# Which engine copies the transposed probabilities in the third attention's loop: two of four on VectorE instead of one of four

## The reference

```python
def _L3_attn_ref(hidden_states, Wq, Wkv, Wo, bo):
    ...
    scores = jnp.einsum('bqhd,bkhd->bhqk', q * scale, k).astype(jnp.bfloat16)
    probs = jax.nn.softmax(scores, axis=-1)
    out = jnp.einsum('bhqk,bkhd->bqhd', probs.astype(jnp.float32), v)
    out = out.astype(jnp.bfloat16)
    out = out.reshape(B, S, H * dh).astype(jnp.float32)
    return out @ Wo + bo
```

## Time and profile before

| what | us |
|---|---|
| median of 3 runs | 673.28 |
| lowest and highest | 672.97 and 673.38 |
| the profiled execution's own time | 673.09 |
| its span (first to last instruction) | 671.3 |
| PE, DVE, ACT, POOL busy in the span | 611.6, 537.1, 398.6, 147.8 |
| copies L1406 on ACT: 24, each | 1.019 |
| copies L1611 on DVE: 8, each | 0.687 |

### The profile page before, as it was taken

How to read it: one execution, slowest core, us unless ns; L and a number is a source line. 1 busy time by engine, 2 the same in 40 slices (tenths; PEclk the granted TensorE clock), 3 DMA queues, 4 the chain that set the end, 5 groups by cost and what they waited for, 6 DMA issues and landing times. The chain is left out here.

```text
span 671.3 us, 9998 instructions
## 1 busy us (share of the span) xinstructions
PE 611.6 (91%) x3186; PEld 483.3 (72%) x3186; DVE 537.1 (80%) x1150; ACT 398.6 (59%) x785; POOL 147.8 (22%) x114
## 2 busy tenths in 40 slices
PE   6998959988899999999998899999857899999996
PEld 4685457785678888887877777777746578888784
DVE  2637589957778877888697799999969689999986
ACT  3523221102878888888864798999953445555552
POOL 0093456656311101111012011111103011111200
PEclk9698597998999999999997555555558889999998
DMA  5000000001312220221000000000001232222210
GB/s 180 1 0 1 0 1 0 1 1 64 109 65 81 96 95 21 73 94 63 0 1 0 1 2 0 0 0 0 1 1 48 82 124 77 101 83 94 83 36 31
DMA packets 9699, 28.78 MB, mean 43 GB/s; under 512 B 960, under 2 KB 3264, under 8 KB 9536
## 3 DMA queue, kind: packets, MB, share of 16 engines
q1 hardware_dynamic: 9664, 28.34, 12.2%
HBM read 27.15 MB, written 1.18 MB: 42 GB/s over the span
## 5 line engine op out<-in xcount | busy, mean ns | idle before, releaser
L1264 DVE TENSOR_TENSOR hL<-hraw,hH 128x1024 fp32r<-128x1024 f32 (+1 forms) x128 | 131.4, 1053 | 33.4 <-ACT hH L1020 32.8
L1090 PE MATMUL ps<-xH,wH 128*128 128x512 f32 x256 | 104.3, 407 | 4.8 <-DVE hraw L1194 3.0
L1024 ACT ACTIVATE hraw<-ps,bias 128x512 f32<-128x512 f32 x128 | 86.6, 686 | 29.3 <-PE ps L1092 24.8
L1091 PE MATMUL ps<-xL,wH 128*128 128x512 f32 x256 | 103.0, 402 | 0.0
L1092 PE MATMUL ps<-xH,wL 128*128 128x512 f32 x256 | 102.8, 402 | 0.0
L955 POOL TENSOR_TENSOR wL<-wraw,wH 128x1024 fp32r<-128x1024 f32 (+1 forms) x16 | 36.4, 2272 | 235.0 <-DVE wH L1141 235.0
L1102 PE MATMUL ps<-hH,wH 128*128 128x512 f32 x192 | 76.2, 397 | 7.3 <-DVE hL L1264 7.3
L1104 PE MATMUL ps<-hH,wL 128*128 128x512 f32 x192 | 76.0, 396 | 0.0
L1103 PE MATMUL ps<-hL,wH 128*128 128x512 f32 x192 | 75.7, 394 | 0.0
L1029 ACT ACTIVATE hraw<-ps 128x512 f32<-128x512 f32 x64 | 38.3, 600 | 52.3 <-PE ps L1092 50.8
L1020 ACT ACTIVATE hH<-hraw 128x1024 fp32r<-128x1024 f32 x64 | 67.5, 1055 | 1.0
(11 more groups left out here) (238 smaller groups left out, 1199.6 us busy)
## 6 DMA issues: line engine op xcount, KB each, us to landing
G<-gates_scratch SPq DMA_DIRECT2D x32, 512.0 KB, 4.7
wraw<-in_ex SPq DMA_DIRECT2D x8, 514.5 KB, 5.4
wraw<-in_ex SPq DMA_DIRECT2D x8, 384.0 KB, 5.6
w<-in_pack SPq DMA_DIRECT2D x1, 1420.5 KB, 7.9
xs<-in_x SPq DMA_DIRECT2D x4, 256.0 KB, 4.7
out<-acc SPq DMA_DIRECT2D x4, 256.0 KB, 2.1
w<-in_pack SPq DMA_DIRECT2D x1, 501.0 KB, 3.8
gates_scratch<-gT SPq DMA_DIRECT2D x4, 32.0 KB
```

Of the source, the lines that this page charges most:

```text
L1024: act.activation(hraw[:, k % 2, h, :], ps[:, h, :], ACT.Gelu, bias=bias[:, place(k, last)[0], h:h + 1]).then_inc(z["act"], 1)
L1090: pe.matmul(o, wH[:, p, at:at + P], xa, start=True, stop=False)
L1091: pe.matmul(o, wH[:, p, at:at + P], xb, start=False, stop=False)
L1264: dve.tensor_tensor(hL[:, k % 2, g * half:(g + 1) * half, :], src, hi.bitcast(F32), ALU.subtract).then_inc(z["hl"], 1)
```

## The change

The copy of step g = 1 (of the pair g = 0) moves from ACT to DVE. DVE then makes the copies of steps 1 and 3, ACT those of steps 0 and 2. On DVE it stands where the other one stands, behind `centre` and ahead of `normalise`. For the very first steps the wait on `op` falls away, since there is nothing before.

```diff
@@ ACT, step
-                if g != 3 and not (first and g == 0):
+                if g in (0, 2) and not (first and g == 0):
                     evacuate(*((b, g - 1) if g else (b - 1, 3)))
@@ DVE, evacuate
                 i = 4 * b + g
                 dve.wait_ge(m3["tp"], i + 1)
-                dve.wait_ge(m3["op"], i - 1)
+                if not (isinstance(b, int) and i < 2):
+                    dve.wait_ge(m3["op"], i - 1)
                 dve.tensor_copy(pT3[:, g % 2].rearrange("p h k n -> p (h k n)"), psb(TB)).then_inc(m3["pt"], 1)
@@ DVE, step
-                if g == 3:
-                    evacuate(b, 2)
+                if g % 2 == 1:
+                    evacuate(b, g - 1)
                 normalise(b, g)
```

## The result

The changed kernel takes 678.69 us in the median of 13 runs (676.13 to 681.05), the kernel before 673.28 us in 13 runs beside it. The ratio is 1.0078, with a 95% interval of 1.0058 to 1.0099: it is slower, by 5.4 us in the medians (3.9 to 6.7 us by the interval), and inside the predicted range of 676.8 to 681.2.

What follows compares the result with a forecast made beforehand. DVE's list was taken to set the pace. Image 0 -0.5, images 1 to 6 +6.4, image 7 +0.6 make +6.5 us on 673.09; with 0.2 for the median, 679.8 us, range 676.8 to 681.2.

Steps and rivals of the forecast that it cites:

- DVE's list sets the pace: From image 0's `lower` to near the last image's end, whatever is added to DVE's list is added to the time.
- The copy costs 0.60 us on DVE: Added copy in each of 8 images: 0.60 us from start to start, bounds 0.60 and 0.69.
- The 0.90 us taken from ACT give nothing back: Step 1: without its 0.90 us copy ACT would stand idle, waiting for DVE's four subtractions, which do not move.
- ACT's new wait: Sign in the changed profile: ACT waits about 0.8 us for L1596 in step 1.
- New stalls under POOL: Step 2, images 1 to 6: DVE comes 0.60 later, POOL stays, adding 0.47 us an image (0 to 0.6).
- The laying out: Step 2's DVE operations placed against POOL's split: `lower` 1.12 us later, 0.60 for the copy and 0.52 of new stalls.
- the upper reading: POOL's first operation at 0.40 us gives 0.52 of new stalls; at 0.49 it gives 0.21; 0.47 was taken.
- One of the signs to look for: In the changed profile, step 2's divisions were to be the group that grew, with the subtractions.
- The first rival, 677.2: Copy costs 0.60 an image but stalls stay as they are: +3.9 us, 677.2 us; chance 17%.
- PE is late: Step 1's later copy delays PE, so `copy_out` and gathers wait 0.1 to 0.3 us in 7 images; up to +2; 10%.
- Image 0 gains 0.5: Image 0: `lower` 0.26 us earlier, plus a POOL stall change of about 0.25 counted as gain: -0.5 (0 to -0.8).
- The sum: Image 0 -0.5, images 1 to 6 +6.4, image 7 +0.6: together +6.5 us, predicted 679.8 us.

Runs made afterwards that it cites:

- The filler: Kernel before, all its copies in place, plus a needless maximum on DVE in step 1 of every image; 676.65 us, ratio 1.0046.
- the relief: Kernel before with ACT's step 1 copy in images 1 to 7 cut to 8 of 1024 columns, DVE's list unchanged; 671.63 us, ratio 0.9995.
- the first four versions: The filler, the relief, and POOL's split spread out in the changed kernel (674.59 us) and in the kernel before (670.41 us).
- the two other faster versions: POOL's split spread out: in the kernel before (ratio 0.9955, second run 0.9931), and with all copies on ACT (0.9942).

## Why the prediction was right, step by step

- *DVE's list sets the pace.* Right. The filler and the relief stand for the two halves of the change; the loop took all of the one (+0.89 for 0.48 of work and 0.41 of stalls) and nothing of the other (15.81 us).
- *The copy costs 0.60 us on DVE.* Right: 0.60 in the trace and 0.62 an image between the two kernels with POOL out of the way.
- *The 0.90 us taken from ACT give nothing back.* Right. ACT's new wait was forecast at about 0.8 and measured 0.59. The idle time counts from the end of `upper` (430.69 + 0.38 = 431.07) to 431.67, while in a row without gaps the exponentials start 0.27 behind `upper`; by that measure it is 0.71. The rest is `upper`, which came 1.09 us behind `rounded` (429.60) and not 0.90, as `upper` did behind the copy in the earlier trace rows.
- *New stalls under POOL.* Right in kind, and nearly in size: 0.47 forecast, 0.44 in the trace of one image, 0.4 as a mean of five. The laying out held operation by operation: the second subtraction, begun at 435.06, ended at 435.76, 0.09 behind POOL's (434.96 + 0.71 = 435.67), the fourth at 436.29 and the first division at 437.04, each 0.08 behind POOL's. The choice near the upper reading was the right one, since POOL's first operation took 0.40. One of the signs to look for was wrong: the divisions of step 2 were to grow as well, and took 1.22 as before. The laying out itself gave them only 434.06 - 432.87 = 1.19 us against 432.94 - 431.81 = 1.13 from start to start, so the sign said more than the working. Moving POOL away removed 0.88 us of the changed kernel's image and 0.49 of the kernel's before; the rest is the copy.
- *The first rival, 677.2.* The whole time does not rule it out: 678.69 lies 1.1 us below the forecast and 1.5 above the rival, and its +3.9 us stand at the very edge of the interval. The periods do: 16.43 was not seen in any run, and POOL did not move along with DVE (3.73 us behind the subtractions, before 3.74).
- *PE is late.* It held nothing up inside the loop: `copy_out` waited not at all in the image shown, and from 382 to 491 the waits view has no wait of DVE for PE behind that of image 0. In the last image, where DVE is not full, the copy of step 3 waited 1.05 us for the transposes, before 0.78:

```profile
504.61 0.69 DVE L1612 COPY pT<-ps 128x1024 bf16<-128x1024 bf16 x1 [1.05 <-PE ps L1478]
```

  The price of this rival does not add up as it stands: 679.8 + 2 is 681.8, not 681.5. Nothing hangs on it.
- *Image 0 gains 0.5.* From DVE's first copy to the first `copy_out` the changed kernel takes 399.81 - 381.87 = 17.94 us:

```profile
381.87 0.69 DVE L1612 COPY pT<-ps 128x1024 bf16<-128x1024 bf16 x1 [2.65 <-PE ps L1478]
382.47 0.17 DVE L1601 RECIPROCAL sm<-smb 128x4 f32<-128x4 bf16 x1
...
383.47 0.41 DVE L1583 SCALAR_TENSOR_TENSOR q3L<-ps,q3H 128x256 fp32r<-128x256 f32 x1
...
399.81 0.29 DVE L1628 COPY oT<-ps 128x256 bf16<-128x256 bf16 x1
```

Before, from the moment the transposes were done (379.71) to `copy_out` at 397.64 it was 17.93. Of the two copies that this stretch holds more than before, that of image 0 fell into what was DVE's wait, and that of image 1 costs 0.60, so the rest gained 0.6. About half of that is the earlier `lower`: 383.47 - 381.87 = 1.60 us behind the transposes, before 381.60 - 379.71 = 1.89, so 0.29 where 0.26 was forecast. The other half is stalls: the divisions beside POOL took 1.49 us before (384.11) and 1.29 after (385.97), and the halved maximum behind them 0.63 and 0.51.
- *The sum.* From the first `copy_out` to the last `add` the time grew from 105.71 to 111.81 us, by 6.1; with nothing from the stretch ahead of it, in which the gain and one copy cancel, the change costs 6.1 us in the trace, where 6.5 were forecast. Five periods of 1.02 more, in place of 1.07, make most of the difference: the term that was a little too large is the new stalls. The last period and the end together grew by 1.0. The measured medians are 5.4 us apart, with an interval that holds both numbers.

The profiled execution itself grew by 8.0 us. The part above 6.1 is not the change's: its transposes of image 0 were done at 381.87 and not at 379.71, some 2.1 us later, ahead of the first moved instruction, and the stage behind the loop was 0.4 us shorter.

## What to carry to other kernels

When several engines are each over 90% busy, look for the one without waits, and give a copy to one that has waits, even if it is slower at it. DVE makes this copy in 0.69 us and ACT in 1.02, and yet the one moved to DVE cost the loop 1.02 us an image, and the one moved to ACT took 0.44 off it, at which point ACT was full. An operation that is put into the list of the pacing engine also moves that list against everything released by the others; what slides under POOL's operations has to be laid out and added. Here it was 0.4 us on top of 0.60.

## What the runs showed of the hardware

- A DVE subtraction or division on bfloat16 that begins while one of POOL's operations runs ends when that one does, 0.08 or 0.09 us past it: so in the image shown before (432.30 against 432.21) and three times in the changed kernel (435.76, 436.29 and 437.04 against 435.67, 436.21 and 436.96). DVE's reductions beside the same POOL operations keep their 0.69 us. Putting POOL's four operations under the reductions took 0.49 us an image from the kernel before and 0.88 from the changed one. The Trainium skill, "SBUF — State Buffer", section "Who interferes with whom", states both sides of this: `tensor_scalar` can be blocked by GpSimd on the shared ports and `tensor_reduce` never is on this chip. The trace agrees with both.
- Whole times scatter more than the first three runs of the kernel before suggested (672.97 to 673.38): all later runs of it but one lie between 668.4 and 676.9 us. The loop does not take part in that. Two profiled executions of the kernel before with POOL spread out have spans of 669.5 and 667.5 us and periods of 15.34 and 15.35; the first `copy_out` is at 399.84 in the one and at 397.72 in the other, so the 2 us arise ahead of it. The stretch from the last `add` to the end varies as well, from 165 to 168 us over the nine traces. PE's granted clock goes with it. Of the runs of the kernel before beside the first four versions, the two shortest (668.41 and 668.71 us) have a mean granted clock of 0.852 and 0.847, two long ones (676.05 and 676.92) 0.834. The two main traces show it in place, before and then after:

```profile
170.00:220.00 50.00, 47.36 (x203) 37.77 (x203) 39.85 (x53) 41.89 (x56) 9.83 (x11) 1.00 0.25 86
365.00:370.00 5.00, 4.44 (x25) 3.47 (x22) 3.30 (x8) 2.82 (x7) 2.38 (x4) 0.50 0.00 0
```

```profile
170.00:220.00 50.00, 47.01 (x191) 36.77 (x190) 38.23 (x52) 38.90 (x53) 10.29 (x12) 0.95 0.24 86
365.00:370.00 5.00, 4.37 (x41) 3.43 (x40) 4.79 (x24) 3.18 (x4) 2.66 (x4) 0.96 0.00 0
```

  In the mixture of experts ahead, from 170 to 220 us, the changed kernel's execution had 0.95 of the full clock and the one before all of it; its last addition there (L1244) starts at 359.1 and not at 354.8, 4.3 us later. At 365 to 370 the later one still has 0.96 and the other is down at 0.50, and by the first transposes the distance is 2.1 us. The program is the same in both up to there. That the clock makes the scatter is argued from this and was not tried; one run of 670.92 us with a mean clock of 0.809 does not fit.
- The version with all copies on ACT is the fastest that was run, 668.17 us, 0.7% below the kernel before (its interval excludes 1) and, by the two ratios (0.9929 / 1.0078), some 1.5% below the changed one. Its interval overlaps those of the two other faster versions, and about half of its gain lies outside the loop, so no order among the three is shown.
